# Four graph layers on one core: row transfers by byte offsets, 17 of the 19 far tiles of edges split between SyncE and ScalarE

## The chip, the core and the metric

The kernel is one program on one core of one Trainium2 chip. The metric is device time in microseconds (us). The core has TensorE (PE), VectorE (DVE), ScalarE (ACT), GpSimd (POOL) and SyncE (SP), each with an instruction stream of its own; they meet only at semaphores. SP and ACT issue transfers from queues of their own (SPq and ACTq in the profile), POOL issues the indirect gathers.

## What is computed

A graph has 3,125 nodes with 128 features and 50,000 edges, sorted by destination. Four layers run one after another, and after each comes the same step, `x = layernorm(x + layer(x))`.

```
L0 (4 steps): m = x @ W_msg.T + b, one row of 128 for each node and edge type
              r = segment_sum(m[src, type4], dst);  x = gru(r, x)
L1:           pe = relu(edge_w @ pos_w1) @ pos_w2
              s = segment_sum(pe * x[src] + x[src], dst); mean over dst; @ sage_w; batchnorm; relu
L2:           r = segment_sum(x[src] @ W_msg.T + emb[type9], dst);  x = gru(r, x)
L3:           graph transformer: 8 heads, keys and values of src, softmax over dst, FFN
```

What matters here is `table[src]` for all edges, once in each step of L0, once in L1 and once in L2: six passes over a table that lies in HBM. L3 has a seventh pass of its own form, which the change leaves alone.

## The kernel before

**Tiles and waves.** The 50,000 edges are 391 tiles of 128; with 12 more for tiles that cross a window of nodes a pass has `P_SLOTS` = 403 tiles. Eight tiles are a wave (`WV`), so a pass has 51 waves, 0 to 50, and the last holds three tiles (`P_LAST`). One `indirect_dma_start` of GpSimd (line 595, `gathers`) fetches the 128 rows of one tile, 512 bytes each, into the buffer `ring`. TensorE sums a tile into its nodes with a matmul against a one-hot matrix that VectorE makes (`pair_hot`, line 1018).

**Near and far tiles.** `ring` has four near places of a wave each (`slot`, the first half of each row of `ring`), in turn. GpSimd may fill a place when TensorE has given a `credit` for the wave four earlier. The other half of `ring` holds far tiles (`far_slot`), up to three waves, which need no turn. `FULL` = 48 is the number of waves (0 to 47) that run in a loop.

**Who fetches what, before.** In the passes of L0 (k = 0 to 3) and of L2 (k = 5) GpSimd gathers 392 tiles in near places and one far tile: 393 gathers. Ten far tiles come row by row: SyncE issues 5 tiles, ScalarE 5 (`far_rows`, line 413), 128 transfers of one row to a tile, 640 each. For eight rows one register load (line 141, `load_rows`) brings eight row numbers; each row then takes three instructions, a fused register operation, a move, and the transfer. In L1 (k = 4) GpSimd gathers all 403 tiles. Over six passes that is 5 x 393 + 403 = 2,368 gathers.

**Order in a pass.** PE and DVE go through waves 0 to 47 and then 49, 50 (far) and 48 (near, gathered last, in two parts of 5 and 3 tiles) in `split_turns`. In L1, `whole_turns` takes waves 0 to 50 in order, and each wave there is a chain in two halves: PE makes the positional term (`L1_pos_w2`), DVE multiplies it into the gathered rows (line 1195, `messages`), PE sums. DVE keeps two one-hot buffers (`OH_BUFS`), so the one-hot of a wave waits for the credit of the wave two before it.

**Start of the program.** The row numbers lie across partitions and are wanted in one partition. SyncE stores them element by element to `xi_dr` (line 496, one store for each of the two tables, 10 columns of 128), waits, and loads them back as one row into `xrow` (line 500). ScalarE waits for that row (`xi_ld`) ahead of `hidden`, whose end PE waits for before it starts the sums of step 0. In the loop of L0, ScalarE issues its rows (`act_rows`) after `hidden` and before `evac`; SyncE issues its rows (`sp_rows`) before the table of the next step. A second load of `xrow`, for the other table, stands behind the output of L0.

Of the kernel before, what the change touches and what calls it, by code (L numbers as in the profile page):

```python
# [19 lines left out]
BF16 = mybir.dt.bfloat16  # L20
# [29 lines left out]
POOL_SLOTS = (FULL + 1) * WV  # L50
LAST_SPLIT = 5
SP_TILES, ACT_TILES = 5, 5
assert POOL_SLOTS + 1 + SP_TILES + ACT_TILES == P_SLOTS and FULL % DEPTH == 0
# [8 lines left out]
FAR = 1.0e6  # L62
# [51 lines left out]
def pair_landed(s):  # L114

    n = len(range(s, P_WAVES, DEPTH))
    return n * 16 * WV - (16 * (WV - P_LAST) if s == (P_WAVES - 1) % DEPTH else 0)


def split_landed(s):  # L120

    return FULL // DEPTH * 16 * WV + (16 * LAST_SPLIT, 16 * (WV - LAST_SPLIT), 0, 0)[s]


def landed_before(k, s):

    if isinstance(k, int) and k > PASS_L1:
        return (k - 1) * split_landed(s) + pair_landed(s)
    return k * split_landed(s)


def landed(k, s, i):

    if isinstance(k, int) and k == PASS_L1 and isinstance(i, int) and i * DEPTH + s == P_WAVES - 1:
        return landed_before(k, s) + pair_landed(s)
# [17 lines left out]
def build(nc, a, out, seen, known):  # L153
    ctx = ExitStack()
    with ctx:
# [148 lines left out]
        x_pl = sem("x_pl")  # L304
        x_sp = [sem(f"x_sp{i}") for i in range(4)]
# [42 lines left out]
        def b_(name):  # L348
# [12 lines left out]
        xrow = rec_flat[0:1, 3600:3600 + (SP_TILES + ACT_TILES) * P].bitcast(I32)  # L361
        t9oh = rec_flat[:, 5024:5024 + WV * NT].bitcast(BF16).rearrange("p (b s c) -> p b s c", b=2, c=NT)
# [3 lines left out]
               .rearrange("p (b s c) -> p b s c", b=2, c=P))  # L366
        cntc, inv = small[:, 208:208 + WIN], small[:, 176:176 + WIN]
# [20 lines left out]

        def split_turns(eng, body):

            with eng.Fori(0, FULL // DEPTH) as i:
                for u in range(DEPTH):
                    body(i, u, i * DEPTH + u, WV)
            for u, (wave, n) in enumerate(((FULL + 1, WV), (FULL + 2, P_LAST), (FULL, WV))):
                body(FULL // DEPTH, u, wave, n)

        def far_slot(t):

            return ring[:, t // WV, t % WV, D:2 * D]
# [7 lines left out]
        def far_rows(eng, which, table, t0, tiles, sems):  # L407

            for t in range(t0, t0 + tiles):
                for q in range(0, P, WV):  # L410
                    r = load_rows(eng, which, xrow, (t - 1) * P + q, table.shape[0] - 1)
                    for j in range(WV):
                        eng.dma_start(far_slot(t)[q + j:q + j + 1, :], table[ds(r[j], 1), :]).then_inc(sems[j % 4], 16)

        def sp_rows(sp, table):

            far_rows(sp, mybir.EngineType.SP, table, 1, SP_TILES, x_sp)

        def act_rows(act, table):

            far_rows(act, mybir.EngineType.Activation, table, 1 + SP_TILES, ACT_TILES, x_ac)

        def far_passes(k):

            return k if isinstance(k, int) and k > PASS_L1 else k + 1

        def far_landed(eng, k):

            eng.wait_ge(x_pl, far_passes(k) * 16)
            for b in range(4):  # L430
                eng.wait_ge(x_sp[b], far_passes(k) * X_SP)
                eng.wait_ge(x_ac[b], far_passes(k) * X_AC)

        def whole_turns(eng, turn):

            with eng.Fori(0, P_TURNS) as i:
                turn(i, DEPTH)
            turn(P_TURNS, P_REST)
# [29 lines left out]
        def _(sp):  # L468
# [25 lines left out]
            sp.wait_ge(s_dv, DV["i_1"])  # L494
            for x_, i_ in zip(xi_dr, (idx4, idx1)):
# [4 lines left out]
            sp.dma_start(xrow, xi_dr[0].rearrange("(a n) -> a n", a=1)).then_inc(xi_ld, 16)  # L500
            sp.wait_ge(xi_ld, 16)
# [19 lines left out]

            rows_out(0)
            far_landed(sp, STEPS - 1)
            sp.dma_start(xrow, xi_dr[1].rearrange("(a n) -> a n", a=1)).then_inc(xi_ld, 16)
            sp.wait_ge(xi_ld, 32)
# [28 lines left out]
        def _(pool):  # L554
# [21 lines left out]
            def gathers(k, table, width, idx):  # L576

                if single(k):
                    waves, deep, slots = WAVES, RING, SLOTS
                elif k == PASS_L1:  # L580
                    waves, deep, slots = P_WAVES, DEPTH, P_SLOTS
                else:
                    waves, deep, slots = FULL + 1, DEPTH, POOL_SLOTS
                for g in range(waves):
# [3 lines left out]
                    if slots == POOL_SLOTS and g == FULL:  # L588
                        pool.indirect_dma_start(
                            far_slot(0), None, table,  # L590
                            bass.IndirectOffsetOnAxis(ap=idx[:, POOL_SLOTS:POOL_SLOTS + 1], axis=0)).then_inc(x_pl, 16)
                    for j in range(min(WV, slots - g * WV)):
                        if slots == POOL_SLOTS and g == FULL and j == LAST_SPLIT:
                            pool.wait_ge(credit, first_wave(k) + DEPTH + FULL + 2 - DEPTH)
                        pool.indirect_dma_start(  # L595
                            rows[:, j, :], None, table,
                            bass.IndirectOffsetOnAxis(ap=idx[:, g * WV + j:g * WV + j + 1], axis=0)
                        ).then_inc(gat[1 if slots == POOL_SLOTS and g == FULL and j >= LAST_SPLIT else u], 16)
# [27 lines left out]
        def _(act):  # L626
# [78 lines left out]
            act.wait_ge(xi_ld, 16)  # L705
# [16 lines left out]
            def relus(i, waves):  # L722
                for u in range(waves):
# [31 lines left out]
            act.wait_ge(xi_ld, 32)  # L755
# [93 lines left out]
        def _(dve):  # L849
# [22 lines left out]
            step("z_base", V.memset(basef[:, :], FAR))  # L872
# [97 lines left out]
            step("w_inv", V.tensor_scalar(offs, ps[0:1, 2, 0:EXTRA], 0.0, FAR, ALU.is_equal, ALU.mult))  # L970
# [22 lines left out]
            step("i_1", V.tensor_copy(idx1[:, :], rec[:, :, F_SRC]))  # L993
            step("i_t9", V.tensor_copy(t9b[:, :], rec[:, :, F_T9]))
# [189 lines left out]
            def messages(i, waves):  # L1184
                for u in range(waves):
                    for hf in range(2):
                        if hf:
                            dve.wait_ge(credit, wave_no(PASS_L1, i, u) + DEPTH)
                            V.tensor_scalar(rts[:, (u + 1) % 2, :], recT[:, ds((i * DEPTH + (u + 1)) * P, P)], 0.0,
                                            None, ALU.add)  # L1190
                            pair_hot(u + 1, i * DEPTH + (u + 1), WV).then_inc(oh_ready, 1)
                        dve.wait_ge(gat[u], landed(PASS_L1, u, i))
                        dve.wait_ge(l1_pe, (i * DEPTH + u) * 2 + (hf + 1))
                        xj = ring[:, u, 4 * hf:4 * hf + 4, 0:D]
# [275 lines left out]
        def _(pe):  # L1470
# [74 lines left out]
            def sums(k, counting=False):  # L1545
                def wave(i, u, g, n):
# [3 lines left out]
                    tail = isinstance(g, int)  # L1550
                    if not tail:
                        pe.wait_ge(gat[u], landed(k, u, i))
                    elif g == FULL + 1:
                        far_landed(pe, k)
                    elif g == FULL:
                        pe.wait_ge(gat[0], landed_before(k, 0) + split_landed(0))
                    pe.wait_ge(oh_ready, oh_no(k, i, u))
                    for j in range(n):
                        if tail and g == FULL and j == LAST_SPLIT:
                            pe.wait_ge(gat[1], landed_before(k, 1) + split_landed(1))  # L1560
                        rows = far_slot((g - FULL - 1) * WV + j) if tail and g > FULL else slot(0 if tail else u)[:, j, :]
                        ins = mm(psf[:, ds(cs[j], PAIR)], rows, pair_oh(u, j), start=False, stop=False)
# [109 lines left out]
            def messages(i, waves):  # L1672
                cs = None
                for u in range(waves):
                    last, cs = cs, load_cols(pe, cols2, i, u, turn=DEPTH)
                    for hf in range(2):
# [7 lines left out]
                        if u or hf:  # L1684
                            u0, h0, c0 = (u, 0, cs) if hf else (u - 1, 1, last)
                            for j in range(4):
                                ins = mm(psf[:, ds(c0[4 * h0 + j], PAIR)], ring[:, u0, 4 * h0 + j, 0:D],
                                         pair_oh(u0, 4 * h0 + j), start=False, stop=False)
# [6 lines left out]
                pe.wait_ge(l1_msg, (i * DEPTH + waves) * 2 + 1)  # L1695
                for j in range(4):
                    ins = mm(psf[:, ds(cs[4 + j], PAIR)], ring[:, waves - 1, 4 + j, 0:D],
                             pair_oh(waves - 1, 4 + j), start=False, stop=False)
# [268 lines left out]
```

## Time and profile before

| what | value |
|---|---|
| time, three runs | median 4402.17 us (4401.73 to 4405.57) |
| the profiled execution | 4408.67 us |
| its span, first to last instruction | 4406.8 us |
| mean granted clock of TensorE | 0.815 of full |
| gathers of GpSimd | 2,784, of which 416 in L3 |
| row transfers | SP 3,200, ACT 3,200 |

The span is what the rows below are read from. Around it lie 1.9 us of the profiled execution. The profiled execution is 6.5 us above the median of the three plain runs. The core is the only one, so there is no other to compare.

How to read it: busy shares are averages over stages. GpSimd is the engine whose gathers fill six of the seven passes; TensorE is busy for 65% of the span, but in most passes it waits for gathered rows. The question for each pass is which wait ends last at its end.

### The profile page before, as it was taken

The numbers are of one execution on the slowest core, as the hardware profiler recorded it, in microseconds if no ns is written. First come the engines' busy times: TensorE is split into PE (matmuls) and PEld (weight loads), VectorE is DVE, ScalarE is ACT, GpSimd is POOL, SyncE is SP. The second block draws the span as 40 slices with busy tenths as digits, with TensorE's granted clock in tenths as the row PEclk, the third lists the DMA queues.
The fourth block names the chain that finished last, engine by engine and source line by source line (L and its number), as shares of the span: only waits on it lengthen the run. The fifth ranks groups of instructions, "written<-read, shape, count | busy, mean of one in ns | idle before, by whom it ended". The sixth has DMA issues, their size and how long they took to land. (4 is left out here: it accounts for less than half of the span.)

```text
span 4406.8 us, 65487 instructions
## 1 busy us (share of the span) xinstructions
PE 2876.3 (65%) x12218; PEld 2170.9 (49%) x12219; DVE 1830.9 (42%) x4838; ACT 421.2 (10%) x690; POOL 2678.7 (61%) x2816
## 2 busy tenths in 40 slices
PE   6555675555765568666677777766557665662687
PEld 3444444444444444444446666544444555652574
DVE  4222252222522226444453333422223666668764
ACT  2000020000200002000021111210001111110334
POOL 3777737777377773777727777367774477771000
PEclk9777797777977779778779999877777888886899
DMA  6222222222222222222212222122221355551340
GB/s 181 55 55 55 53 84 55 55 54 52 84 55 55 54 52 83 55 55 54 52 31 52 52 52 52 27 58 55 55 53 32 104 154 156 156 156 47 114 133 15
DMA packets 157822, 314.71 MB, mean 71 GB/s; under 512 B 58069, under 2 KB 79004, under 8 KB 157086
## 3 DMA queue, kind: packets, MB, share of 16 engines
q0 software_dynamic: 95744, 209.89, 18.4%
q1 hardware_dynamic: 55454, 101.15, 6.6%
q10 hardware_dynamic: 6400, 1.65, 0.2%
q14 instruction: 203, 1.66, 0.1%
q8 instruction: 21, 0.34, 0.0%
HBM read 250.84 MB, written 61.64 MB: 71 GB/s over the span
## 5 line engine op out<-in xcount | busy, mean ns | idle before, releaser
L595 POOL DMA_INDIRECT ring<-m_tab,idx x1568 | 1488.6, 949 | 720.1 <-issue 601.0
L1480 PE MATMUL ps<-oh,ring 128*128 128x256 f32 (+1 forms) x3328 | 963.6, 451 | 485.7 <-DMA ring<-m_tab,idx 380.6
L1480 PE MATMUL ps<-nodes,ring 128*128 128x256 f32 x2350 | 808.5, 509 | 475.1 <-DMA ring<-m_tab,idx 363.3
L1480 PEld LDWEIGHTS ps<-oh,ring 128*128 128x128 f32 x3328 | 703.2, 241 | 630.8 <-issue 528.0
L595 POOL DMA_INDIRECT ring<-x_tab,idx x795 | 754.9, 950 | 254.7 <-issue 244.3
L1480 PEld LDWEIGHTS ps<-nodes,ring 128*128 128x128 f32 x2350 | 575.6, 259 | 617.2 <-issue 516.4
L1018 DVE TENSOR_SCALAR oh<-iota,dl 128x256 f32<-128x256 f32 x1248 | 380.2, 375 | 951.4 <-PE ps L1480 943.3
L1018 DVE TENSOR_SCALAR nodes<-iota,dl 128x256 f32<-128x256 f32 x1183 | 361.8, 376 | 831.6 <-PE ps L1480 829.0
L595 POOL DMA_INDIRECT ring<-kv_tab,idx x416 | 399.2, 960 | 148.7 <-issue 126.5
L605 POOL TENSOR_TENSOR small<-small,bc 128x4 f32<-128x4 f32 (+1 forms) x28 | 31.1, 1109 | 597.4 <-DVE small L1118 597.4
L1480 PE MATMUL ps<-wpad,rts 128*128 128x128 f32 x832 | 162.8, 376 | 195.9 <-DVE pw L1270 195.9
L1480 PE MATMUL ps<-nodes,wt 128*128 128x512 f32 (+1 forms) x532 | 236.5, 586 | 52.9 <-ACT rec L672 16.3
L1480 PEld LDWEIGHTS ps<-wpad,rts 128*128 128x128 f32 x832 | 149.2, 278 | 208.0 <-DVE pw L1270 208.0
L658 ACT ACTIVATE nodes<-ps 128x512 f32<-128x512 f32 x18 | 9.5, 598 | 2428.2 <-PE ps L1480 2428.2
L1195 DVE SCALAR_TENSOR_TENSOR ring<-ps,ring 128x512 f32<-128x512 f32 x102 | 70.6, 692 | 324.0 <-DMA ring<-x_tab,idx 166.6
L1480 PEld LDWEIGHTS ps<-nodes,wt 128*128 128x128 f32 x532 | 100.3, 201 | 178.9 <-issue 117.9
L1480 PE MATMUL ps<-rts,wpad 128*128 128x128 f32 x816 | 118.9, 290 | 105.8 <-DVE ring L1195 105.8
L1025 DVE TENSOR_TENSOR oh<-cst,dl 128x256 f32<-128x256 f32 x416 | 148.7, 420 | 51.9 <-PE ps L1480 51.9
L1480 PEld LDWEIGHTS ps<-rts,wpad 128*128 128x128 f32 x816 | 100.6, 194 | 125.1 <-DVE ring L1195 120.6
L1480 PEld LDWEIGHTS ps<-rec,pw 128*128 128x128 bf16 x806 | 97.3, 121 | 97.0 <-issue 48.7
L1269 DVE TENSOR_TENSOR ring<-ring,ps 128x512 f32<-128x512 f32 x104 | 71.2, 684 | 169.8 <-DMA ring<-kv_tab,idx 169.8
L1480 PE MATMUL ps<-nodes,rec 128*128 x832 | 123.4, 312 | 0.0
(248 smaller groups left out, 2432.1 us busy)
## 6 DMA issues: line engine op xcount, KB each, us to landing
ring<-m_tab SPq DMA_DIRECT2D x2560, 0.5 KB
ring<-m_tab ACTq DMA_DIRECT2D x2560, 0.5 KB
ve_dr<-pw SPq DMA_DIRECT2D x52, 512.0 KB, 2.9
ring<-ve_dr SPq DMA_DIRECT2D x52, 512.0 KB, 3.4
ring<-m_tab,idx POOLq DMA_INDIRECT x1572, 2.6
m_tab<-ring SPq DMA_DIRECT2D x75, 256.0 KB, 2.2
ring<-x_tab,idx POOLq DMA_INDIRECT x796, 2.4
ring<-x_tab SPq DMA_DIRECT2D x640, 0.5 KB
```

What stands on the lines that cost most here:

```text
L595: pool.indirect_dma_start(rows[:, j, :], None, table, bass.IndirectOffsetOnAxis(ap=idx[:, g * WV + j:g * WV + j + 1], axis=0)).then_inc(ga ...
L605: nc.gpsimd.tensor_tensor(rs[:, ws], sd[:, ws], b_("minus_half").to_broadcast([P, CH[c][1] // P]), ALU.pow).then_inc(ln_r, 1)
L658: nc.scalar.activation(gT[:, c0:c0 + cw], ps[:, c, 0:cw], ACT.Copy).then_inc(ev_a, 1)
L1018: ins = V.tensor_scalar(pair_oh(u, j), iota2[:, :], dl2[:, ds(wave * WV + j, 1)], None, ALU.is_equal)
L1025: ins = V.tensor_tensor(oh[:, v, j:j + 2, :], iota.unsqueeze(1).to_broadcast([P, 2, P]), dl[:, ds((i * RING + (u + ahead)) * WV + j, 2)].u ...
L1195: V.scalar_tensor_tensor(xj, ps[:, 7, :].rearrange("p (s d) -> p s d", d=D), 1.0, xj, ALU.add, ALU.mult).then_inc(l1_msg, 1)
L1269: V.tensor_tensor(kj, kj, pe_, ALU.add).then_inc(a_kv, 1)
L1480: return T.matmul(o, lhsT, rhs, start=start, stop=stop, skip_group_check=True)
```

## The change

It does five things.

1. **Byte offsets.** The row numbers are shifted left by 9 on VectorE before they are stored (`i_x0`, `i_x1`, two operations on 17 columns), so that what is loaded into a register is an offset in bytes. `far_rows` views the table and the place as bytes and uses the register as it is. One register load brings 16 offsets in place of 8.
2. **Shares.** A pass has 19 far tiles (waves 48, 49, 50). SyncE fetches 8 of them in all six passes, L1 too; ScalarE fetches 9 in L0 and L2. GpSimd gathers the 384 near tiles and 2 far ones, 386; in L1, where ScalarE fetches none, 384 + 11 = 395. Over six passes: 5 x 386 + 395 = 2,325 gathers.
3. **Order.** The loop runs 11 turns of four waves (0 to 43). Then come waves 44, 45, 46, 48, 49, 50 and 47 (`LAST_POS`), in every pass, L1 too. GpSimd gathers its far tiles after wave 43, then 44 to 47; the last three tiles of 47 have a semaphore of their own (`gat_end`).
4. **Row numbers.** There are 17 columns of 128 in each of two stores in place of 10, and two loads (`row_numbers`), one row for SyncE and one for ScalarE. ScalarE waits for both (`xi_ld` 32). The second pair is loaded before the output of L0.
5. **Places.** `t9oh` moves to the end of `gT`, since the rows of numbers are longer.

```diff
-POOL_SLOTS = (FULL + 1) * WV
+NEAR = FULL * WV
+FAR = P_SLOTS - NEAR
-SP_TILES, ACT_TILES = 5, 5
+SP_TILES, ACT_TILES = 8, 9
+POOL_FAR = FAR - SP_TILES - ACT_TILES
+L1_FAR = FAR - SP_TILES
+LOOPED = FULL // DEPTH - 1
+ROW = 4 * D
...
-        xrow[0:1, start:start + WV], engines=[which], min_val=0, max_val=hi,
+        xrow[0:1, start:start + 2 * WV], engines=[which], min_val=0, max_val=hi,
...
+        LAST_POS = (*range(LOOPED * DEPTH, FULL - 1), *range(FULL, P_WAVES), FULL - 1)
...
+        def row_numbers(eng, j):
+            for to, (a0, n) in zip(xrow, ((0, SP_TILES), (SP_TILES, ACT_TILES))):
+                eng.dma_start(to, xi_dr[j].rearrange("(a n) -> a n", a=1)[:, a0 * P:(a0 + n) * P]).then_inc(xi_ld, 16)
...
+            flat = table.rearrange("n d -> (n d)").bitcast(U8)
             for t in range(t0, t0 + tiles):
-                for q in range(0, P, WV):
-                    r = load_rows(eng, which, xrow, (t - 1) * P + q, table.shape[0] - 1)
-                    for j in range(WV):
-                        eng.dma_start(far_slot(t)[q + j:q + j + 1, :], table[ds(r[j], 1), :]).then_inc(sems[j % 4], 16)
+                to = far_slot(POOL_FAR + t)
+                for q in range(0, P, 2 * WV):
+                    r = load_rows(eng, which, rows, (t - t0) * P + q, (table.shape[0] - 1) * ROW)
+                    for j in range(2 * WV):
+                        eng.dma_start(to[q + j:q + j + 1, :].bitcast(U8),
+                                      flat[ds(r[j], ROW)].rearrange("(a n) -> a n", a=1)).then_inc(sems[j % 4], 16)
...
-                sp.dma_start(x_.rearrange("(k p) -> p k", p=P), i_[:, POOL_SLOTS + 1:P_SLOTS],
+                sp.dma_start(x_.rearrange("(k p) -> p k", p=P), i_,
...
+            far_landed(sp, STEPS - 1)
+            row_numbers(sp, 1)
+            sp.wait_ge(xi_ld, 64)
             rows_out(0)
+            for c in range(2):
+                sp.wait_ge(ln_dma[c], LN_DMA(1, c))
+            sp_rows(sp, x_tab[0])
             rows_out(1)
...
+                    if slots == NEAR and g == LOOPED * DEPTH - 1:
+                        far = [*range(POOL_FAR)]
+                        if k == PASS_L1:
+                            far += range(POOL_FAR + SP_TILES, FAR)
...
-            act.wait_ge(xi_ld, 16)
+            act.wait_ge(xi_ld, 32)
...
+            for n, (to, i_) in enumerate(zip(x_bytes, (idx4, idx1))):
+                step(f"i_x{n}", V.tensor_scalar(to, i_[:, NEAR + POOL_FAR:P_SLOTS], 9, None, ALU.logical_shift_left))
```

## Rows read from the trace of the kernel before

**Rows 1.** The page, the chain that ended last, shares of the span.
```profile
POOL 24%; PE 10%; issue 9%; DVE 3%; DMA 1%; ACT 1%; DVEq 0%; ACTq 0%
```
**Rows 2.** Gather windows, step 0, L1, L2: length, busy PE PEld DVE ACT POOL, PEclk, DMA.
```profile
58.60:549.50 490.90, 288.26 (x815) 217.23 (x815) 125.08 (x404) 8.93 (x18) 371.31 (x392) 0.75 0.24 54
2292.80:2797.70 504.90, 381.62 (x2368) 338.05 (x2367) 191.84 (x543) 59.11 (x99) 382.39 (x403) 0.98 0.20 52
2878.20:3369.30 491.10, 294.18 (x833) 219.13 (x832) 114.91 (x379) 10.70 (x20) 371.55 (x393) 0.75 0.21 54
```
**Rows 3.** Timeline of POOL, step 0: the 33rd gather, first of wave 4.
```profile
99.16 0.94 POOL L595 DMA_INDIRECT ring<-m_tab,idx  x1 [0.30 <-issue]
```
**Rows 4.** Timeline of PE, end of step 0: waves 47, 49, 50, 48.
```profile
541.01 6.72 PE L1480 MATMUL ps<-nodes,ring 128*128 128x256 f32 x16 [2.88 <-DVE oh L1018]
547.57 3.62 PE L1480 MATMUL ps<-oh,ring 128*128 128x256 f32 x16
551.02 1.46 PE L1480 MATMUL ps<-nodes,ring 128*128 128x256 f32 x6
553.54 3.71 PE L1480 MATMUL ps<-oh,ring 128*128 128x256 f32 x16 [1.07 <-DVE oh L1018]
```
**Rows 5.** Timeline of DVE, same end: the one-hot of wave 48.
```profile
551.22 2.19 DVE L1018 TENSOR_SCALAR oh<-iota,dl 128x256 f32<-128x256 f32 x8 [2.58 <-PE ps L1480]
```
**Rows 6.** Timeline of PE, end of step 3: first matmuls of waves 49 and 50.
```profile
2210.93 0.68 PE L1480 MATMUL ps<-oh,ring 128*128 128x256 f32 x2
...
2215.47 0.68 PE L1480 MATMUL ps<-nodes,ring 128*128 128x256 f32 x2
```
**Rows 7.** Chain in order of time, L1 (start us, us, what).
```profile
2749.13 3.79 PE ps L1480 x24
...
2767.38 3.79 PE ps L1480 x24
...
2793.94 2.54 DMA ring<-x_tab,idx
2796.50 0.70 DVE ring L1195
...
2811.28 2.00 PE ps L1480 x8
```
**Rows 8.** Timeline of SP, start of the program.
```profile
55.19 1.25 SPq L496 DMA_DIRECT2D xi_dr<-idx  x2
77.86 0.24 SPq L500 DMA_DIRECT2D rec<-xi_dr  x1
```
**Rows 9.** DMA packets from 56 to 78 us.
```profile
DMA packets 2869, 0.57 MB, mean 26 GB/s; under 512 B 2699, under 2 KB 2699, under 8 KB 2868
```
**Rows 10.** Timelines of ACT's rows (step 0, L2) and PE's first sum.
```profile
90.27 330.33 ACTq L413 DMA_DIRECT2D ring<-m_tab  x640
...
2901.53 328.58 ACTq L413 DMA_DIRECT2D ring<-x_tab  x640
...
91.28 3.72 PE L1480 MATMUL ps<-oh,ring 128*128 128x256 f32 x16
```
**Rows 11.** Timeline of ACT, four row transfers of one batch.
```profile
200.32 1.32 ACTq L413 DMA_DIRECT2D ring<-m_tab  x4
```
**Rows 12.** Instructions of lines 413, 141 and 86 (ns min/median/max).
```profile
L413 ACTq FUSED_REGOPS  x3200: 37/37/43, 90.1 to 3229.8; - x189
L413 ACTq MOVE ring<-m_tab x2560: 29/29/29, 90.2 to 2056.0; - x197
L413 ACTq DMA_DIRECT2D ring<-m_tab x2560: 213/213/1587, 90.3 to 2056.1; - x197
L141 ACTq TENSOR_LOAD <-rec x400: 714/830/1019, 89.4 to 3226.1; - x134
L86 PEldq TENSOR_LOAD <-cols x513: 586/591/976, 89.9 to 4294.6; - x171
L86 PEldq TENSOR_LOAD <-cols x1: 787/787/787, 547.2 to 547.2; - x1
```

More of the change, by code:

```diff
@@ L366, in build @@
                .rearrange("p (b s c) -> p b s c", b=2, c=P))
+        x_bytes = [pw[:, 1, 32 * j:32 * j + SP_TILES + ACT_TILES].bitcast(I32) for j in range(2)]
         cntc, inv = small[:, 208:208 + WIN], small[:, 176:176 + WIN]
@@ L387, in slot, with tiles_of @@
             return ring[:, s % RING, :, h:h + D]
+        LAST_POS = (*range(LOOPED * DEPTH, FULL - 1), *range(FULL, P_WAVES), FULL - 1)
+        def tiles_of(wave):
+            return P_LAST if wave == P_WAVES - 1 else WV
         def split_turns(eng, body):
-            with eng.Fori(0, FULL // DEPTH) as i:
+            with eng.Fori(0, LOOPED) as i:
                 for u in range(DEPTH):
                     body(i, u, i * DEPTH + u, WV)
[L394 to L399, printed above, removed]
+            for p, wave in enumerate(LAST_POS):
+                body(LOOPED, p, wave, tiles_of(wave))
         X_SP, X_AC = (n * P // 4 * 16 for n in (SP_TILES, ACT_TILES))
@@ L405, in far_slot, with wave_rows @@
             return ring[:, t // WV, t % WV, D:2 * D]
-        def far_rows(eng, which, table, t0, tiles, sems):
-            for t in range(t0, t0 + tiles):
-                for q in range(0, P, WV):
-                    r = load_rows(eng, which, xrow, (t - 1) * P + q, table.shape[0] - 1)
-                    for j in range(WV):
-                        eng.dma_start(far_slot(t)[q + j:q + j + 1, :], table[ds(r[j], 1), :]).then_inc(sems[j % 4], 16)
+        def wave_rows(wave, u):
+            if isinstance(wave, int) and wave >= FULL:
+                return ring[:, wave - FULL, :, D:2 * D]
+            return slot(wave % DEPTH if isinstance(wave, int) else u)
@@ new lines, in arrived, with all_arrived @@
+        def arrived(eng, k, i, u, wave):
+            if not isinstance(wave, int):
+                eng.wait_ge(gat[u], landed(k, u, i))
+            elif wave == FULL:
+                far_landed(eng, k)
+            elif wave == FULL - 1:
+                eng.wait_ge(gat[DEPTH - 1], landed_before(k + 1, DEPTH - 1))
+            elif wave < FULL:
+                eng.wait_ge(gat[wave % DEPTH], landed_before(k + 1, wave % DEPTH))
+        def all_arrived(eng, k):
+            eng.wait_ge(gat_end, (k + 1) * (16 * (WV - LAST_SPLIT)))
@@ L434, in whole_turns @@
         def whole_turns(eng, turn):
-            with eng.Fori(0, P_TURNS) as i:
-                turn(i, DEPTH)
-            turn(P_TURNS, P_REST)
+            with eng.Fori(0, LOOPED) as i:
+                turn(i, [i * DEPTH + u for u in range(DEPTH)])
+            turn(LOOPED, LAST_POS)
         block = ctx.enter_context(nc.Block())
@@ L493, in _ @@
             table(0, m_rows, 512, tb0)
-            sp.wait_ge(s_dv, DV["i_1"])
-            for x_, i_ in zip(xi_dr, (idx4, idx1)):
-                sp.dma_start(x_.rearrange("(k p) -> p k", p=P), i_[:, POOL_SLOTS + 1:P_SLOTS],
+            sp.wait_ge(s_dv, DV["i_x1"])
+            for x_, i_ in zip(xi_dr, x_bytes):
+                sp.dma_start(x_.rearrange("(k p) -> p k", p=P), i_,
                              allow_slow_non_contiguous=True).then_inc(xi_st, 16)
@@ L499, in _ @@
             sp.wait_ge(s_pe, PE["dT"])
-            sp.dma_start(xrow, xi_dr[0].rearrange("(a n) -> a n", a=1)).then_inc(xi_ld, 16)
-            sp.wait_ge(xi_ld, 16)
+            row_numbers(sp, 0)
+            sp.wait_ge(xi_ld, 32)
             for s in range(STEPS):
@@ L576, in gathers @@
             def gathers(k, table, width, idx):
[L578 to L583, printed above, removed]
+                waves, deep, slots = (WAVES, RING, SLOTS) if single(k) else (FULL, DEPTH, NEAR)
                 for g in range(waves):
@@ L597, in gathers @@
                             bass.IndirectOffsetOnAxis(ap=idx[:, g * WV + j:g * WV + j + 1], axis=0)
-                        ).then_inc(gat[1 if slots == POOL_SLOTS and g == FULL and j >= LAST_SPLIT else u], 16)
+                        ).then_inc(gat_end if slots == NEAR and g == FULL - 1 and j >= LAST_SPLIT else gat[u], 16)
+                    if slots == NEAR and g == LOOPED * DEPTH - 1:
+                        far = [*range(POOL_FAR)]
+                        if k == PASS_L1:
+                            far += range(POOL_FAR + SP_TILES, FAR)
+                        for t in far:
+                            pool.indirect_dma_start(
+                                far_slot(t), None, table,
+                                bass.IndirectOffsetOnAxis(ap=idx[:, NEAR + t:NEAR + t + 1], axis=0)).then_inc(x_pl, 16)
             def norm(ln):
@@ L722, in relus @@
             def relus(i, waves):
-                for u in range(waves):
+                for u in range(len(waves)):
                     for hf in range(2):
@@ L754, in _ @@
             hidden(STEPS, "L2")
-            act.wait_ge(xi_ld, 32)
+            act.wait_ge(xi_ld, 64)
             for c in range(2):
@@ L871, in _ @@
             step("z_recT", V.memset(recT[:, WAVES * P:(WAVES + 1) * P], 0.0))
-            step("z_base", V.memset(basef[:, :], FAR))
+            step("z_base", V.memset(basef[:, :], FAR_AWAY))
             dve.wait_ge(s_edge, 80)
@@ L1184, in messages @@
             def messages(i, waves):
-                for u in range(waves):
+                for u, wave in enumerate(waves):
                     for hf in range(2):
                         if hf:
+                            ahead = waves[u + 1] if u + 1 < len(waves) else i * DEPTH + (u + 1)
                             dve.wait_ge(credit, wave_no(PASS_L1, i, u) + DEPTH)
[L1189 to L1192, printed above, removed]
+                            V.tensor_scalar(rts[:, (u + 1) % 2, :], recT[:, ds(ahead * P, P)], 0.0, None, ALU.add)
+                            pair_hot(u + 1, ahead, WV).then_inc(oh_ready, 1)
+                        arrived(dve, PASS_L1, i, u, wave)
+                        if hf and isinstance(wave, int) and wave == FULL - 1:
+                            all_arrived(dve, PASS_L1)
                         dve.wait_ge(l1_pe, (i * DEPTH + u) * 2 + (hf + 1))
-                        xj = ring[:, u, 4 * hf:4 * hf + 4, 0:D]
+                        xj = wave_rows(wave, u)[:, 4 * hf:4 * hf + 4, :]
                         V.scalar_tensor_tensor(xj, ps[:, 7, :].rearrange("p (s d) -> p s d", d=D), 1.0, xj,
@@ L1549, in wave @@
                     c16 = load_cols(pe, cols16, 0, g, (WIN - 1) * NT, n=n) if counting else None
[L1550 to L1556, printed above, removed]
+                    arrived(pe, k, i, u, g)
                     pe.wait_ge(oh_ready, oh_no(k, i, u))
                     for j in range(n):
[L1559 to L1562, printed above, removed]
+                        if isinstance(g, int) and g == FULL - 1 and j == LAST_SPLIT:
+                            all_arrived(pe, k)
+                        ins = mm(psf[:, ds(cs[j], PAIR)], wave_rows(g, u)[:, j, :], pair_oh(u, j), start=False, stop=False)
                         if counting:
@@ L1673, in messages @@
                 cs = None
-                for u in range(waves):
-                    last, cs = cs, load_cols(pe, cols2, i, u, turn=DEPTH)
+                for u, wave in enumerate(waves):
+                    last, cs = cs, load_cols(pe, cols2, 0, wave)
                     for hf in range(2):
@@ L1694, in messages @@
                         ins.then_inc(l1_pe, 1)
-                pe.wait_ge(l1_msg, (i * DEPTH + waves) * 2 + 1)
+                end = len(waves) - 1
+                pe.wait_ge(l1_msg, i * (2 * DEPTH) + (2 * len(waves) + 1))
                 for j in range(4):
-                    ins = mm(psf[:, ds(cs[4 + j], PAIR)], ring[:, waves - 1, 4 + j, 0:D],
-                             pair_oh(waves - 1, 4 + j), start=False, stop=False)
+                    ins = mm(psf[:, ds(cs[4 + j], PAIR)], wave_rows(waves[end], end)[:, 4 + j, :],
+                             pair_oh(end, 4 + j), start=False, stop=False)
                 ins.then_inc(credit, 1)
```

51 lines of the change are left out of this document (19 added, 32 removed).

## The prediction, made before the changed kernel ran

> **What bounds the kernel now.** I read the page first. The chain that ended last is mostly gathers of GpSimd and their issue gaps [rows 1], so the question is what a pass costs and what ends it. The windows from first to last gather come next [rows 2]: in step 0, 393 gathers start over 490.9 us, 1.252 us apart (490.9 / 392), in L1 403 over 504.9 us (1.256), in L2 1.253. PE is busy 288 of 491 us in step 0, but 382 of 505 in L1, where DVE and ACT have work in each wave too: L1 has little room. Then the end of a pass, in the timelines. In step 0 the last gather starts at 549.50 [rows 2], yet PE ends at 553.54 + 3.71 = 557.25 [rows 4]. That end hangs on the chain from wave 47: PE takes it at 541.01, at low speed first (6.6 us until 547.57), then 49 (3.45 to 551.02), 50, and then it waits for DVE, which starts the one-hot of wave 48 only when 49 is done [rows 5]. So the last gather isn't what ends a pass, and a gather saved isn't 1.25 us saved. I work out each end instead.
>
> **Fewer gathers, ends of L0 and L2.** The tail is now 46, 48, 49, 50, 47 where it was 47, 49, 50, 48. Wave 46's last gather is the 378th where wave 47's was the 384th: six gathers earlier, 6 x 1.252 = 7.5 us. One more full far wave lies in the chain behind it, 3.45 us (551.02 - 547.57 [rows 4]). Wave 47 is the 386th gather, 10.0 us after the 378th, while PE comes to it after 6.6 + 3.45 + 3.45 + 2.5 = 16.0 us; it doesn't wait for it. So each of steps 0, 1, 2 and L2 gains 7.5 - 3.45 = 4.06 us, and not the 8.8 us of seven gathers: -16.3 us in four passes. Step 3 counts as well, and a full wave costs 2215.47 - 2210.93 = 4.54 us there [rows 6]: -3.0 us.
>
> **End of L1.** Here a wave is a chain PE, ACT, PE, DVE in halves of (2767.38 - 2749.13) / 4 = 4.56 us when nothing is waited for [rows 7], so 9.1 us a wave against 10.05 us of gathers. Before, wave 49 lands at 2793.94 + 2.54 = 2796.48 and PE ends at 2813.28, 16.8 us later, with waves 49 and 50 (four halves) in it. Now waves 46, 48, 49, 50, 47 stand there, ten halves. Wave 46's last gather is the 387th (352 + 11 + 24), wave 49's was the 400th: 13 x 1.256 = 16.3 us earlier. Six halves more are 27.4 us. L1 ends 27.4 - 16.3 = +11.1 us later, though it has eight gathers less. The far rows cover nothing there: they are in place early, but their work is kept for the end.
>
> **The start.** The stores to `xi_dr` go from 2 x 10 to 2 x 17 columns of 128 elements of 4 bytes. Before, they are issued at 55.19 and SP goes on at 77.86 [rows 8]; in those 22 us the queues move 2,699 packets under 512 bytes [rows 9], the 2,560 elements among them. Some 21 us scale with the elements: x 0.7 = +14.5 us (rounded down a little; from 0, if the time were fixed, to 15.5). Behind this wait stand SP's loads of the row, and behind `xi_ld` ACT's `hidden`, behind that PE's first sums, 91.28 [rows 10] -> 105.8. GpSimd's 33rd gather needs wave 0's credit, 3.7 us later: 109.6. It was at 99.16, held by nothing but the issue gap [rows 3]. So the whole of step 0 moves by +10.4 us; the 4.2 us of cover before it (95.0 to 99.16) are used up. The two shifts on DVE and the second short load (0.24 us to issue) lie inside this. The loads before the output of L0 are hidden by the gate and norm work behind step 3, since SP has no other work then.
>
> **The row transfers.** A row's pitch on ACT is (1.32 - 0.213) / 3 = 0.369 us [rows 11]: three instructions of 37, 29 and 213 ns [rows 12] and three gaps of 30. The fused register operation makes row number into offset; without it 0.302 us. (If the move goes too: 0.243; I keep it, since nothing in it depends on the row number's scale.) The 640 rows took 330.33 us and the first load 0.84: 4.14 us for eight. A batch of 16 then is 4.14 - 8 x 0.067 + 8 x 0.302 + what a load of 16 costs above one of 8. No row shows such a load. From below: nothing. From above: twice the load, +0.83 us. A load of three took 787 ns where one of eight takes 591 [rows 12], so number alone doesn't set it, and a second access costs about 0.2; I take 0.19. That is 6.21 us, x 72 batches = 447 us for ACT's 1,152 rows. SP has 1,024 rows and no `hidden` ahead of them, so ACT is the later one.
>
> In step 0 ACT begins at 90.27 - 0.8 + 14.5 = 104.0 and is done at 551; landed, an estimate, 1.3 us later (a whole gather takes 2.54 [rows 7]): 552.3. PE asks for it after wave 46: 58.6 + 377 x 1.252 + 2.6 + 10.4 + 0.3 + 6.7 = 550.6. So PE waits 1.7 us and restarts at low speed (wave 47 shows 6.6 us where 49 takes 3.45 [rows 4]; I take 1.3 us of it): +3. In L2 the run starts at 2901.53 and is landed by 3349, wanted at 2878.2 + 377 x 1.253 + 2.6 + 7 = 3360: hidden with 11 us to spare. Steps 1 to 3 have no store ahead of them; I take them as no tighter than L2.
>
> The Trainium skill (Runtime: NRT & Kernel Launch, Instruction fetch mechanics) speaks against the long load: it says that a register load costs about 200 ns a register even in bulk. This trace disagrees: eight registers take 830 ns on ACT and 591 on PE. By the page a load of 16 would be 3.2 us, 72 of them some 157 us a pass more than I take, and the kernel, an estimate, near 5100 us.
>
> **Sum.** +10.4 - 16.3 - 3.0 + 11.1 + 3 = +5.2 us. The profiled execution, 4408.7 (span 4406.8 and 1.9 around it), would become 4413.9; it stands 6.5 above the median, so the median goes from 4402.2 to 4407.4 us. Under 0.2% (8.8 us) either way can't be told from no change.
>
> **Rivals.**
> - *ACT's rows late in step 0.* If the load of 16 costs 0.3 us more than one of eight, ACT is done 8 us later and PE waits for all of it; with two or three microseconds in the other terms (they are ends of chains) the sum is +14: 4416 us. For it: the margin of step 0 is already below zero. Against: L2's margin. It decides from about +7 us of wait. Chance 0.27.
> - *A load that goes with its registers, or arithmetic that stays.* Twice the load: +46 us a pass, 49 in step 0, 35 in L2, about 25 each in steps 1 to 3 (an estimate, at most L2's 35), in all +161: 4563 us. If the fused operation stays, 77 us a pass, some +310: 4715. For it: ACT's rows would bound every pass. Against: 787 ns for three registers; an offset in bytes needs no factor. Chance 0.11.
> - *Faster: the gathers are what counts.* 43 gathers x 1.253 = 54 us saved, less 13 at the start: 4361 us. It holds if PE were through with 46, 48, 49 and 50 within the 10 us in which wave 47 is gathered. Against: 16 us in step 0 [rows 4] and 36 in L1 [rows 7]. For it: [rows 1] only. Chance 0.10.
> - *The store's time is fixed* and not by its elements: then neither start nor wait costs, 5.2 - 13.4 = -8: 4394 us, at the bound. Against: [rows 9]. Chance 0.07, half of it faster.
> - My forecast: 0.45.
>
> **How the numbers follow.** Predicted 4407, the likeliest case. Range 4396 to 4424: it takes in the late rows and most of the fixed store, and leaves out the long load (0.11) and the gathers' case (0.10). Of the likeliest alone: 4400 to 4413. Slower by over 0.2%: 0.27 + 0.11 = 0.38. Within: 0.45 + 0.04 = 0.49. Faster: 0.10 + 0.03 = 0.13.
>
> **What would show it.** In the profile after: SP's load of the row numbers near 92 instead of 77.86; the 33rd gather near 110; no FUSED_REGOPS at the row transfers, MOVE still there; loads near 1.0 us on ACT; ACT's rows of step 0 done near 551; PE ending step 0 some 9 us later than before, steps 1 and 2 some 4 us shorter from first gather to end, and L1 11 us longer with its last five waves back to back and no DMA wait among them. The prediction is wrong if the store lands early, if the far waves run faster than 3.45 us, or if DVE, ACT and PE pass a wave of L1 in less than 9.1 us.

## The result, and the profile after

The changed kernel takes 4539.68 us (median of 4 runs, 4536.52 to 4544.29), the kernel before 4403.03 us beside it: a ratio of 1.031, 95% interval 1.0293 to 1.0328. That is 136.7 us slower. I had said 4407, in a range of 4396 to 4424. The profiled execution has a span of 4538.9 us.

The page of the changed kernel, the chain that ended last, by engine and by line:

```profile
POOL 14%; PE 11%; ACTq 9%; issue 8%; DVE 4%; DMA 1%; ACT 1%; DVEq 0%
POOL ring L612 14%; PE ps L1510 10%; ACTq L420 7%; ACTq L131 2%; DVE ring L1225 1%; DMA ring<-x_tab,idx 0%; POOL small L630 0%; PE ps L1628 0%; POOL ring L621 0%; DVE ring L1341 0%; DVE ring L1388 0%; DVE nodes L1342 0%; DVE nodes L1389 0%; PE ps L1833 0%; DMA kv_tab<-ring 0%
```

ACTq, ScalarE's queue, stood at 0% [rows 1]. Now 9% of the chain are its row transfers (L420) and the loads of their numbers (L131). So the reader looks for a wait on rows. The waits of PE give one for each pass with rows (line waited for: us in all, times, longest); steps 0 to 3, then L2, each line from its own window:

```profile
PE ps L1510 <- DMA ring<-m_tab: 38.9, 1, 38.9
PE ps L1510 <- DMA ring<-m_tab: 19.6, 1, 19.6
PE ps L1510 <- DMA ring<-m_tab: 21.9, 1, 21.9
PE ps L1510 <- DMA ring<-m_tab: 18.5, 1, 18.5
PE ps L1510 <- DMA ring<-x_tab: 32.9, 1, 32.9
```

Together 131.8 us: nearly the whole loss of 136.7. (L1 has no such wait; it is treated below.) Where it stands in a pass, PE's timeline at the end of step 0 shows, waves 46, 48, 49, 50, 47:

```profile
542.02 3.72 PE L1510 MATMUL ps<-oh,ring 128*128 128x256 f32 x16 [3.11 <-DMA ring<-m_tab,idx]
584.62 5.59 PE L1510 MATMUL ps<-nodes,ring 128*128 128x256 f32 x16 [38.89 <-DMA ring<-m_tab]
590.05 3.62 PE L1510 MATMUL ps<-oh,ring 128*128 128x256 f32 x16
593.51 1.46 PE L1510 MATMUL ps<-nodes,ring 128*128 128x256 f32 x6
596.03 3.72 PE L1510 MATMUL ps<-oh,ring 128*128 128x256 f32 x16 [1.07 <-DVE oh L1046]
```

Set beside [rows 4], the chain behind the wait is the one that I described, wave by wave 3.45 us. The wait in front of wave 48 is the new thing. ScalarE's timeline says why: its last rows go out until 583.30.

```profile
500.07 83.23 ACTq L420 DMA_DIRECT2D ring<-m_tab  x203
```

The instructions of the two lines (ns min/median/max, first and last start) answer to [rows 12]: the fused operation is gone, MOVE is still there, a transfer still has its median of 213 or 214 ns, and a load of 16 takes 1302 ns on ACT.

```profile
L420 ACTq MOVE ring<-m_tab x4608: 29/29/30, 93.1 to 2297.0; - x192
L420 ACTq DMA_DIRECT2D ring<-m_tab x4608: 213/214/742, 93.2 to 2297.0; - x192
...
L131 SPq TENSOR_LOAD <-rec x384: 1132/1232/1441, 82.6 to 3407.5; - x192
L131 ACTq TENSOR_LOAD <-rec x360: 1182/1302/1570, 91.9 to 3483.0; - x180
```

The start, against [rows 8] and [rows 3]; SP's timeline, POOL's at the 33rd gather, and PE's first sum:

```profile
55.56 1.81 SPq L521 DMA_DIRECT2D xi_dr<-pw  x2
79.81 0.55 SPq L410 DMA_DIRECT2D rec<-xi_dr  x2
```
```profile
99.17 0.94 POOL L612 DMA_INDIRECT ring<-m_tab,idx  x1 [0.30 <-issue]
```
```profile
93.80 1.56 PE L1510 MATMUL ps<-oh,ring 128*128 128x256 f32 x6
```

The row load comes 1.95 us later than before, not 14.5, and the 33rd gather stands where it stood. The windows from first to last gather (step 0, L1, L2: length, busy PE, PEld, DVE, ACT, POOL, PEclk, DMA) show GpSimd starting its gathers undisturbed, 1.25 us apart, as in [rows 2]:

```profile
58.70:540.70 482.00, 277.78 (x777) 208.28 (x775) 122.33 (x392) 9.36 (x18) 364.49 (x386) 0.73 0.30 55
2380.80:2875.30 494.50, 369.92 (x2265) 327.04 (x2264) 183.26 (x517) 56.75 (x95) 374.33 (x395) 0.96 0.21 54
2978.30:3460.20 481.90, 282.71 (x804) 210.23 (x802) 116.51 (x376) 10.12 (x19) 364.40 (x386) 0.76 0.27 55
```

And the end of L1, PE's timeline, every other of its halves:

```profile
2873.24 1.13 PE L1510 MATMUL ps<-rts,wpad 128*128 128x128 f32 x8 [0.94 <-DVE ring L1225]
...
2882.62 1.13 PE L1510 MATMUL ps<-rts,wpad 128*128 128x128 f32 x8 [0.97 <-DVE ring L1225]
...
2891.81 1.13 PE L1510 MATMUL ps<-rts,wpad 128*128 128x128 f32 x8 [0.88 <-DVE ring L1225]
...
2901.00 1.13 PE L1510 MATMUL ps<-rts,wpad 128*128 128x128 f32 x8 [0.88 <-DVE ring L1225]
...
2910.34 1.99 PE L1510 MATMUL ps<-oh,ring 128*128 128x256 f32 x8 [0.96 <-DVE ring L1225]
```

Waves back to back, no wait on a DMA, 9.3 us each. From first gather to the next pass's first gather, L1 takes 597.4 us (2380.8 to 2978.3) where it took 585.4 [rows 2]: +12.0.

### The profile page after: what moved, and what is told of

The parts are those of the page before. It is cut to its first block and busy times, and to the rows that moved or that the text cites. A ratio compares the mean times of both kernels' runs of the same rounds, so it can differ in the third digit from the quotient of the medians.

```text
span 4538.9 us, 69601 instructions
## 1 busy us (share of the span) xinstructions
PE 2879.6 (63%) x12218; PEld 2172.4 (48%) x12219; DVE 1836.0 (40%) x4840; ACT 421.3 (9%) x690; POOL 2637.5 (58%) x2773
## 3 DMA queue, kind: packets, MB, share of 16 engines
q14 instruction: 238, 1.95, 0.1%
## 5 line engine op out<-in xcount | busy, mean ns | idle before, releaser
L612 POOL DMA_INDIRECT ring<-m_tab,idx x1536 | 1458.8, 950 | 812.7 <-issue 462.7
L612 POOL DMA_INDIRECT ring<-x_tab,idx x768 | 728.1, 948 | 245.7 <-issue 227.6
L1510 PEld LDWEIGHTS ps<-nodes,pw 128*128 128x128 bf16 x806 | 95.5, 118 | 93.2 <-issue 43.9
```

The source lines that it names most:

```text
L612: pool.indirect_dma_start(rows[:, j, :], None, table, bass.IndirectOffsetOnAxis(ap=idx[:, g * WV + j:g * WV + j + 1], axis=0)).then_inc(ga ...
L1510: return T.matmul(o, lhsT, rhs, start=start, stop=stop, skip_group_check=True)
```

## The experiments

The first four ran on a chip on which the kernel before takes 6162.86 us instead of 4403, so their times answer another question (they are told last). Three were run again, e4's order as part of e6; beside these later runs the kernel before took 4402.5 to 4405.9 us.

**e5: ScalarE 8 tiles.**

```diff
-SP_TILES, ACT_TILES = 8, 9
+SP_TILES, ACT_TILES = 8, 8
```

> The same kernel as e1 (ScalarE 8 tiles, GpSimd 387 gathers), to be run where the kernel before takes its usual 4403 us: there it took 6163 us, with pauses of 0.7 us between the instructions of SyncE and ScalarE which neither trace shown so far has. Theory, ScalarE's rows are what every pass of the changed kernel ends with: 64 batches of 6.82 us are issued by 528 us in step 0, no wait for rows is left, about 4410 us. Rival, the end of a pass is late for another reason: above 4470 us.

Measured: 4402.02 us, 0.9995 of the kernel before (0.9985 to 1.0005). One tile of 128 rows is worth 137.7 us. PE's timeline at the end of step 0 has no wait for rows left; ScalarE issues its last row at 533.7:

```profile
542.83 3.71 PE L1510 MATMUL ps<-oh,ring 128*128 128x256 f32 x16 [2.98 <-DMA ring<-m_tab,idx]
546.39 3.62 PE L1510 MATMUL ps<-nodes,ring 128*128 128x256 f32 x16
549.84 3.62 PE L1510 MATMUL ps<-oh,ring 128*128 128x256 f32 x16
553.29 1.46 PE L1510 MATMUL ps<-nodes,ring 128*128 128x256 f32 x6
555.82 3.71 PE L1510 MATMUL ps<-oh,ring 128*128 128x256 f32 x16 [1.07 <-DVE oh L1046]
```

With the wait gone, the other terms can be read. From first gather to the next pass's, steps 0 to 3, L1 and L2 differ from the kernel before by -0.5, -4.9, -3.8, -6.5, +13.3 and -1.5 us. Each is a difference of two single executions. How far to trust it shows in e8 (below), which leaves order and shares as they were: there the same six differ by -3.0, +0.4, -0.3, -6.8, -0.5 and -2.9. So the gains of steps 1 and 2 and the loss of L1 stand out; those of steps 0, 3 and L2 don't.

**e6: the same, and layer one in another order.** GpSimd's eleven far gathers go behind wave 44, and the waves are taken as 44, 48, 49, 50, 45, 46, 47.

```diff
+        L1_POS = (LOOPED * DEPTH, *range(FULL, P_WAVES), *range(LOOPED * DEPTH + 1, FULL))
...
-            turn(LOOPED, LAST_POS)
+            turn(LOOPED, L1_POS)
...
-                    if slots == NEAR and g == LOOPED * DEPTH - 1:
+                    if slots == NEAR and g == LOOPED * DEPTH - (k != PASS_L1):
```

> ScalarE 8 tiles (as e5), and layer one with the far gathers behind wave 44 and the waves in the order 44, 48, 49, 50, 45, 46, 47 (as e4). Theory, layer one's end is ten halves of some 4.56 us behind the landing of wave 46: taken early, the far waves fill a time in which PE waits for gathers, PE is through 24.6 us after the last landing instead of 35.6, 11 us less than e5: 4391 us, 0.997 of the kernel before. Rival, layer one hangs on its gathers or on SP's far rows: no less than e5, 4402.

Measured: 4389.27 us, 0.9971 (0.996 to 0.9982): 0.3% below the kernel before, a small gain, and under 1 over its whole interval. PE starts its last matmuls of L1 at 2795.00, 26.8 us behind the start of the last gather (2768.2), where the changed kernel had 35.1 (2910.34 - 2875.2).

```profile
2795.00 1.99 PE L1512 MATMUL ps<-oh,ring 128*128 128x256 f32 x8 [0.96 <-DVE ring L1227]
```

L1 takes 588.2 us to the next pass's first gather, 10.5 less than in e5: the order of the waves was the cost in L1.

**e7: loads of 32** (shares 8 and 9).

```diff
-        xrow[0:1, start:start + 2 * WV], ...
+        xrow[0:1, start:start + 4 * WV], ...
```

> As e2, where the kernel before takes its usual time: the changed kernel (shares 8 and 9) with loads of 32 numbers. Theory, a load is a fixed part and about 59 ns a register: 2.25 us for 32, a batch of 32 some 12.8 us for 13.64, 30 us less a pass; step 0 waits some 9 us for rows, L2 some 3, steps 1 to 3 not: near 4425 us. Rival, 32 registers cost more than in proportion (over 2.6 us): no gain, 4520 us or above.

Measured: 4518.25 us, 1.0263 (1.0248 to 1.0278). The load is as foretold, the batch isn't: 13.6 us on ACT, and PE still waits 32.0 us in step 0.

```profile
L131 SPq TENSOR_LOAD <-rec x192: 2025/2125/2298, 78.5 to 3387.6; - x192
L131 ACTq TENSOR_LOAD <-rec x180: 2140/2250/2414, 87.3 to 3457.2; - x180
```

Neither theory says that. Transfers themselves had become longer. In the changed kernel, line 420 from 93 to 250 us (first two lines) and from 320 to 500 (last two):

```profile
L420 SPq DMA_DIRECT2D ring<-m_tab x385: 224/225/283, 92.9 to 249.9; - x193
L420 ACTq DMA_DIRECT2D ring<-m_tab x383: 213/214/742, 93.2 to 249.7; - x192
...
L420 SPq DMA_DIRECT2D ring<-m_tab x408: 224/225/570, 319.8 to 499.8; - x136
L420 ACTq DMA_DIRECT2D ring<-m_tab x403: 213/226/532, 319.9 to 499.8; - x135
```

768 rows in 157 us are 4.89 a microsecond for the two queues together; 811 in 180 us are 4.51, and on SP transfers of up to 570 ns appear. And e7 from 320 to 500 us, with half as many loads:

```profile
L420 SPq DMA_DIRECT2D ring<-m_tab x407: 224/261/559, 319.9 to 499.9; - x136
...
L420 ACTq DMA_DIRECT2D ring<-m_tab x404: 213/258/520, 320.0 to 499.5; - x135
```

811 in 180 us again. What the load saves, the transfers take back: there is a ceiling of 4.5 rows a microsecond. It needs both queues. In L1 SyncE issues its 1,024 rows alone, beside the same gathers, and there the long load does pay; SP's timeline in e7, step 0 and L1:

```profile
80.62 435.81 SPq L420 DMA_DIRECT2D ring<-m_tab  x1024
...
2367.30 404.69 SPq L420 DMA_DIRECT2D ring<-x_tab  x1024
```

404.69 us are 12.65 for a batch of 32, near the 12.8 foretold. Nor is it the supply of instructions: in the kernel before an engine ran 25 of them in a batch of 4.14 us, 6.0 a microsecond, in the changed one 33 in 6.82, 4.8.

The increments of the gathers' semaphores show that a backlog builds up, of transfers that are issued and not yet done. A wave brings 128 increments. In the changed kernel's step 0, up to 8 of them, one in sixteen, come late: the last 5.3 us behind the start of the wave's last gather at 138 us, 8.7 at 188, 11.8 at 238, and some 16 from 338 on. In the kernel before all 128 are there after some 2.6 us, 3.6 at most from 100 us on, and so they are in L1 of the changed kernel and of e7, where one queue issues alone.

The rows lag too: the trace has two increments for a row, one some 0.4 us after its issue and one when it has landed, and this second one comes some 2 us after the issue at first, some 15 from 350 us on and 1.2 for ScalarE's last rows, when SyncE has long finished.

**e8: byte offsets alone**, in the kernel before (shares 5 and 5, loads of 8, its own order).

```diff
-                    r = load_rows(eng, which, xrow, (t - 1) * P + q, table.shape[0] - 1)
+                    r = load_rows(eng, which, xrow, (t - 1) * P + q, (table.shape[0] - 1) * ROW)
                     for j in range(WV):
-                        eng.dma_start(far_slot(t)[q + j:q + j + 1, :], table[ds(r[j], 1), :])
+                        eng.dma_start(far_slot(t)[q + j:q + j + 1, :].bitcast(U8),
+                                      flat[ds(r[j], ROW)].rearrange("(a n) -> a n", a=1))
```

> As e3, where the kernel before takes its usual time: byte offsets alone, shares 5 and 5, loads of 8. Theory, a batch of 8 goes from 4.13 to 3.59 us and nothing else changes; the rows were never waited for: within 4 us of 4403. Rival, two queues at 4.46 rows a microsecond collide as in the changed kernel (a transfer of SP over 300 ns in 8 of 100, 4096-byte packets with a 95th percentile of 668 ns instead of 387): seen in the trace, and if a pass felt it, above 4412.

Measured: 4403.05 us, 1.0004 (0.9995 to 1.0013). A batch of 8 takes 3.62 us, ScalarE's rows of step 0 are out at 379.4 instead of 420.4, and nobody had waited for them. The rival's signs are absent: no gather lands late (3.6 us at most), and on SP (100 to 375 us) no transfer is longer than 278 ns. So describing rows in bytes is not the trouble; at this pitch the two queues issue 4.5 rows a microsecond together, just the ceiling, and build no backlog.

```profile
L417 SPq DMA_DIRECT2D ring<-m_tab x594: 224/225/278, 99.9 to 357.9; - x198
```

**e10: is the ceiling one of bytes?** e7 with half of each row left out.

```diff
-                        eng.dma_start(to[q + j:q + j + 1, :].bitcast(U8), flat[ds(r[j], ROW)] ...
+                        eng.dma_start(to[q + j:q + j + 1, 0:D // 2].bitcast(U8), flat[ds(r[j], ROW // 2)] ...
```

> As e7 (loads of 32, shares 8 and 9), but each row transfer of SyncE and ScalarE fetches only the first 256 of its 512 bytes, so half of each of their far rows is missing from the sums. In e7 the two queues together issued 5.1 rows a microsecond at first and 4.51 from 320 us on. Theory, the two queues share something that takes a fixed time for each transfer, whatever its bytes: 4.5 again from 320 us, a batch of 32 still 13.5 us on the mean, the time near 4518. Rival, the ceiling is one of bytes: half the bytes lift it, 5.1 a microsecond throughout, a batch of 32 near 12.7 us, ScalarE's rows done 29 us earlier in step 0, the time near 4430 us.

Measured: 4502.96 us in one run, a batch of 32 at 13.4 us, and from 320 to 500 us 813 rows, 4.52 a microsecond. The ceiling counts transfers, not bytes. The bytes weigh a little all the same: this run keeps 5.06 a microsecond until 250 us, where e7 has fallen to 4.76 from 200 to 250, and it is 15 us below e7's median. It is one run, but e7's four lie within 8 us.

```profile
L420 SPq DMA_DIRECT2D ring<-m_tab x411: 224/233/626, 320.1 to 498.7; - x137
L420 ACTq DMA_DIRECT2D ring<-m_tab x402: 213/244/712, 319.9 to 498.2; - x134
```

**e11: loads of 8** (shares 8 and 9), `2 * WV` in the load and in the loop replaced by `WV`.

> The changed kernel with loads of 8 row numbers instead of 16, shares 8 and 9 as they are. Theory, below the ceiling of some 4.5 rows a microsecond a batch of 8 takes 3.62 us as in e8: 144 of them 521 us instead of 491, each of the five passes 30 us longer, near 4690 us, and no gather's landing late. Rival, since the ceiling and not the load holds the changed kernel back, short loads cost little: 5 to 10 us a pass, under 4600 us.

Measured: 4686.29 us, 1.0645 (1.0627 to 1.0663), and no gather lands late (3.2 us at most from 100 to 500 us of step 0). A batch of 8 is 3.62 us, 7.24 for 16 rows where the changed kernel takes 6.82; ScalarE's rows of step 0 end at 612.5. Loads of 16 gain 146.6 us at these shares; they were not what was wrong with the change. The run also shows what the backlog costs the gathered waves. PE takes wave 46 of step 0 at 534.28 here and at 542.02 in the changed kernel, with the same order and the same gathers:

```profile
534.28 6.38 PE L1510 MATMUL ps<-oh,ring 128*128 128x256 f32 x16 [6.19 <-DMA ring<-m_tab,idx]
```

The loads of 8:

```profile
L131 SPq TENSOR_LOAD <-rec x768: 683/784/1004, 81.6 to 3545.4; - x192
L131 ACTq TENSOR_LOAD <-rec x720: 718/827/1071, 90.9 to 3638.1; - x180
```

**e9: all three**: the order of e6, loads of 32 as in e7, SyncE 9 tiles and ScalarE 8.

> Layer one ordered as in e6, loads of 32, SyncE 9 tiles and ScalarE 8, so GpSimd gathers 386 tiles a pass and 394 in layer one. Theory, with loads of 32 SP's nine tiles take 36 x 12.6 us and are issued by 538 us in step 0, just before PE wants them; a gather less a pass brings wave 46 forward by 1.25 us: 4391 - 5 x 1.25 = 4385 us. Rival, the rows are late again, by up to 10 us a pass: 4400 to 4430.

Measured: 4467.94 us, 1.0147 (1.0134 to 1.016): the rival, and more of it than the rival said. It ran beside e7, and its expectation knows no ceiling. SP's nine tiles take 13.7 us a batch and end at 572.3. 17 tiles are 2,176 rows, at 4.51 some 482 us, however they are shared out; 16 tiles are 454. The faster first 200 us take some 12 us off either (an estimate: the changed kernel has issued 1,932 rows by 500 us). PE wants the rows some 460 us after SP starts, so by this estimate no share of 17 tiles would have been in time in step 0 (470 us at best).

**e1 to e4: the first round**, on the slow chip: e1 is the kernel of e5, e2 that of e7, e3 that of e8, e4 the changed kernel with the order of e6 in layer one.

> The changed kernel with one tile less for ScalarE: 8 instead of 9, so GpSimd gathers 387 tiles and not 386. Theory, rows of ScalarE are what every pass ends with: a batch of 16 rows takes 6.82 us there, so 64 batches take 436 us instead of 491, and in step 0 the last row is issued near 528 us, before PE is through with wave 46 at 545.5. The waits for rows (38.9, 19.6, 21.9, some 14 and 32.9 us) and the restarts at low speed go, five gathers of 1.25 us come: about 4410 us. Rival, the changed kernel is late because of something else in its end of a pass (the order 46, 48, 49, 50, 47, or gathers landing late): then at least half of the 137 us stays, above 4470 us.

> The changed kernel with loads of 32 row numbers instead of 16, shares 8 and 9 as they are. Theory, a load has a fixed part and about 59 ns a register (8: 0.83 us, 16: 1.30): 32 cost some 2.25 us, and a batch of 32 takes some 12.8 us against 13.64 for two of 16; 30 us less a pass, step 0 still waits some 9 us and L2 some 3, together near 4425 us. Rival, a long load costs more than in proportion, or 32 registers at once are held back: 2.6 us or more for a load, no gain, 4520 us or above.

> The kernel before with the byte offsets alone: shares 5 and 5, loads of 8, its own order of waves. Theory, byte offsets save the fused operation and nothing else: a batch of 8 goes from 4.13 to 3.59 us, the rows were done 120 us before they are wanted, so the time stays within 4 us of 4403. Rival, transfers described in bytes cost more or disturb the gathers, since two queues then issue 4.5 rows a microsecond: transfers of 450 ns on SP as well as on ACT, late packets of gathers, and a time above 4412.

> The changed kernel with another order in layer one alone: far gathers behind wave 44 instead of 43, waves taken as 44, 48, 49, 50, 45, 46, 47. Theory, the end of layer one is ten halves of 4.56 us behind wave 46, and the far waves fill time in which PE waits for gathers when they are taken early: PE ends 24.6 instead of 35.6 us after the last landing, 11 us less, about 4529 us. Rival, the time of layer one is set by its gathers or by the far rows that SP fetches: no gain, 4540.

Measured there: 6572.56, 6597.81, 5730.65 and 6693.36 us, against 6162.86: ratios of 1.0666 (1.0642 to 1.0689), 1.0695 (1.0668 to 1.0723), 0.929 (0.9268 to 0.9312) and 1.0856 (1.0833 to 1.088). None of the expectations is decided by that; each was written for a chip at 4403. The same edits come out otherwise there: e1 is 6.7% slower than the kernel before where e5 is level, e3 7.1% faster where e8 is level. Row transfers of e3 from 100 to 400 us, to be held against those of e8 (same code):

```profile
L417 ACTq MOVE ring<-m_tab x225: 3/29/728, 111.0 to 399.9; - x113
L417 ACTq DMA_DIRECT2D ring<-m_tab x225: 4/248/1403, 111.1 to 400.0; - x113
```

Rows go out at a third of the pace of e8 (225 in 289 us; there 605 in 274), with pauses of 0.7 us between instructions: 257 of over 0.5 us on SyncE in 400 us (e1), 184 us in all, where the changed kernel's trace has none. No gather is late there. I take it that SyncE and ScalarE are short of instructions on that chip, not of DMA; no run shows where the pauses come from.

## Why the prediction was wrong, step by step

- **The step that failed: "That is 6.21 us, x 72 batches = 447 us for ACT's 1,152 rows."** It is 6.82 us, 491 us. Two terms of it were too small. *The load of 16* was taken at +0.19 us over one of eight; it costs 1.30 - 0.83 = +0.47, so 72 x 0.28 = 20 us. By 8, 16 and 32 (0.83, 1.30, 2.25 us) a load has a fixed 0.36 and 59 ns a register. I had drawn "a second access costs about 0.2" from two loads on PE; the bounds held (0 to +0.83), the choice in them was too low. The Trainium skill's 200 ns a register (Runtime: NRT & Kernel Launch, Instruction fetch mechanics) is not borne out, as I said; but its direction, that bulk doesn't make registers free, was the better hint. *The rows themselves* were given 0.302 us each, as if 17 tiles went as smoothly as ten. In the first 150 us a batch is 6.59 us, 0.1 above 6.21 + 0.28; later the two queues meet the ceiling and the mean rises to 6.82: 72 x 0.33 = 24 us, of which 7 stood before the ceiling was felt. Nothing in my account had the two queues limiting each other. The split into 20 and 24 is bookkeeping, for under the ceiling a cheaper load hardly helps: e7 spends 36 x (2 x 1.30 - 2.25) = 12.6 us less on ScalarE's loads in a pass, and its rows of step 0 go out in 485 us instead of 490.
- **"In L2 ... hidden with 11 us to spare", "steps 1 to 3 ... no tighter than L2".** 44 us more a pass turn 11 us of cover into PE's wait of 32.9 in L2, and into 18.5 to 21.9 in steps 1 to 3. The second rival, a load that goes with its registers (4563 us, chance 0.11), had this chain and nearly this time; its cause, the load, is 20 of the 44 us. My first rival, a load 0.3 us above one of eight, was too small as well: it is 0.47 above, and that rival charged step 0 alone. None of my rivals had rows that get dearer when both queues are busy.
- **The start, +10.4: wrong, nothing.** SP's load comes 1.95 us later for 70% more elements. The elements are moved soon after issue (in the kernel before some 2,600 packets of 4 bytes within 4 us, in the changed one some 4,400 within 12), but the increments of the second store come only at 75.5 to 77.8 us (75.8 to 79.8 in the changed kernel). So the rival "the store's time is fixed" was right for this term, though why the report takes so long no run shows. [rows 9] counted packets over 22 us, but not when within them they moved. Since ACT began 12 us earlier than I said, this hid part of the error in the rows: its rows still ended 32 us late.
- **The tails of L0 and L2, -4.06: right in steps 1 and 2, not shown elsewhere.** e5 shows -4.9 and -3.8 in steps 1 and 2, e6 -5.7 and -3.6, each with one gather more than the changed kernel. In step 3 (-6.5) and L2 (-1.5, -3.8) the gain can't be told from what e8 has without any change of order (-6.8, -2.9). Step 0 gives only -0.5 and -2.1, and here the backlog is the reason: wave 46's last gather starts at 530.63 in the changed kernel and PE gets to the wave at 542.02, waiting for a DMA; in e11, which has no late gather, it gets there at 534.28. In steps 1 and 2 of e5 and e6 the last row is out some 30 us before the wave, so the backlog is gone, and its gathers land after 2.5 us. The gathers' rival (4361) is out: no run gained 1.25 us for each gather saved.
- **The end of L1, +11.1: right.** +12.0 in the changed kernel, +13.3 in e5, and e6 takes 10.5 of it back by the order alone. e7, e10 and e11 have +12.2, +13.4 and +11.8. No wait for a DMA among the last five waves, as said.
- **What stays open.** A gather is reported by 16 increments; that one of the sixteen is late, by the same 15 or 16 us as the rows, suggests that all single rows go through one of the 16 DMA engines, which the gathers use as well. The trace names no engine, and no run had the two queues without gathers; the ceiling is shown, its place is argued.

## What to carry to other kernels

When work is moved from a shared engine to queues of row transfers, the price of a row taken under a light load is a lower bound: count the transfers of all queues together, look for a rate above which they no longer scale, and see how much cover the last one has in every pass, not in one. Where cover is a few microseconds of 450, an error of 0.3 us in a batch decides; try one unit less before judging the idea (here one tile made 137.7 us). Work kept for the end of a pass is paid in full, though its data came early; put it where the engine waits anyway.

## What the runs showed of the hardware that was not expected

- Single-row transfers of two hardware queues together went no faster than 4.5 a microsecond beside the gathers once a backlog stood (the changed kernel, e7, e10), with 512 or 256 bytes each. SyncE alone, in L1, issued 2.44 a microsecond without a hold-up (2.53 with loads of 32). At 4.9 a microsecond the backlog grew for some 200 us before the issuing engines felt it; one in sixteen of the gathers' increments then came some 16 us after the gather's start (up to 19.6 in e10).
- A register load: 0.83, 1.30 and 2.25 us for 8, 16 and 32 registers on ScalarE, 0.78, 1.23 and 2.13 on SyncE.
- The two stores of 4-byte elements took 22 us to be reported for 2,560 elements and 24 us for 4,352, though their packets had moved within 4 and 12 us.
- The same kernel before took 6163 us on one chip and 4403 on another. On the chip with the pauses byte offsets alone, one instruction less a row, gave 7.1% (0.929), on the other nothing (1.0004).
